# Fused tokenizer, attention and FFN: leaky ramps in one ScalarE instruction, queries placed by on-chip transfers, group loop unrolled, new order and banks

## The chip, the cores and the metric

The kernel runs on one core of a Trainium2 chip. A core has TensorE (PE), VectorE (DVE), ScalarE (ACT), GpSimd (POOL) and SyncE (SP, which here only issues transfers). The metric is the device time of one execution in microseconds, median of several runs.

## The reference, cut to what matters

64 images of 3 x 84 x 84 and 64 texts of 77 x 192 come in; the output has 64 x 102 x 192. For each image:

```python
h = leaky_relu(batchnorm(conv2d(x, stem_w, stem_b, 4)))      # 96 x 21 x 21, slope 0.01
offset = conv2d(h, off_w, off_b, 4)                          # 32 x 5 x 5
h = leaky_relu(batchnorm(deform_conv(h, offset, dcn_w, dcn_b)))   # bilinear samples: 25 tokens of 192
h = concatenate([h, txt])                                    # 102 tokens of 192
h = h + quantised_attention(layernorm(h))                    # 12 heads of 16, 8-bit q, k, v;
                                                             # softmax as integer exponential, probabilities powers of two
h = h + gelu(layernorm(h) @ in_w + in_b) @ out_w             # 768 hidden
```

`leaky_relu(x)` is x where x is at least 0 and 0.01 x elsewhere.

## The kernel before, in words

Images are worked on in 16 groups of four (`GRP`). Each engine runs a list of its own, written out by hand in the string `SLOT`: an entry such as `dve.STEM.3` reads engine, stage, lag, and means that in slot s the engine does this stage for image s - 3. All entries stand in one part of a slot of four, so one pass over the list serves one group; in a pass, stages of several groups are mixed. A lag counts only within its engine: there is no barrier between engines, which meet at semaphores alone. Stages in `PER_GROUP` are done once per group. The entries of one engine are executed strictly in their order, so an instruction that waits holds up all behind it. `walk` emits the passes: those up to slot 27 written out, then eight turns of a hardware loop (`Fori`, with counts computed from a register), then the rest written out.

The stages, in the order that a group goes through them:

- LX loads patches; STEM0 and STEM1 (PE, line 1089) are the first convolution of two images each. ACT's `stem` (line 571) writes 0.01 x the result to `LK`, DVE's `stem` (line 846) writes the maximum of the two to `H`.
- HTT transposes `H` in four pieces (L1095), OFF and OFS give the sampling offsets (L1111, L1118), POOL splits and masks them (OFS, RX; L511 to L532). HAT on PE (L1127, L1129), ACT (L601, L604) and DVE (L856) and HATW (L861) turn them into bilinear weights. INT (L1138, copied out at L613) samples. DCN (L1151) is the product with the second convolution's weights: ACT's `dcn` (L620) scales by 0.01 into `LKD`, DVE's `dcn` (L870) takes the maximum into `TOKB`, and SP stores it to a DRAM scratch (L472).
- LA loads tokens and texts into `XA`; LN1, RS1 and LN1X normalise (L883 to L902, L550), the product with the weights for v is V0 and V1 (L1171, L1174, rounded at L644), for q and k FQ0 and FQ1 (L1198, L1204, rounded at L652, L654).
- QKC on DVE (`qk_cast`, lines 919 to 937) casts q to `QB` and k to `KK`, then builds the block matrix `Q0`/`Q1`: twelve `tensor_scalar` multiply all rows of q by a column of `own` that is 1 in the rows of one head and 0 elsewhere. SC on PE multiplies by `KK` (L1215, L1218) and waits for it.
- The softmax goes between ACT (SC L664, SQ L671, LOG L678, PR L686), DVE (SC, MAX, BND, QQ, QQG, REM, EP, EXP, SUM, RCP, PW, PR; L943 to L1026) and POOL (MAX, L542).
- PV1, PV2, PV3 are the probabilities' transposition, product with v and output projection (L1230, L1239, L1249), RES the residual (L1045) on `XR`, loaded by LR; LN2, LN2X, FFN0 to FFN2 and FF2 the second half (L1182, L1186, L1264, L1052); YO0 and YO1 store the output.

PSUM has eight banks: two for the scores and six shared by all other products by the table `BANKS`; before PE writes to one, `BankUse.take` makes it wait until the bank's last result has been read. DVE also prepares weights in the head: `sampling_constants` after the fourth STEM, then behind the first four HATW in turn `fold_bn2`, `scalars`, `qkv_integers`, `qkv_weights`, and `proj_weights` behind the first DCN.

Of the kernel before, what the change touches and what calls it, by code (L numbers as in the profile page):

```python
# [65 lines left out]
dve.SUM.15 act.LN1X.10 pe.FF2.21 dve.RCP.15 act.HTT.5 dve.REM.14 pe.PV3.19 dve.EP.14 act.LN1X.9  # L66
pool.RX.4 pe.PV2.17 dve.HAT.8 act.PV2.12 dve.BND.13 pe.HAT.10 dve.HATW.8 act.LN1X.8 dve.QQ.13
sp.LA.12 pe.FF2.20 act.STEM.2 dve.EXP.14 dve.QQG.13 pe.PV3.18 act.V.11 dve.EP.13 pe.LN1X.15
act.HTT.4 dve.REM.13 dve.SUM.14 pool.RS2.12 act.V.10 pe.HTT.9 dve.V.13 dve.RCP.14 act.FQ0.8
pe.PV1.16 dve.PW.15 act.FQ1.8 dve.SC.12 pe.LN1X.14 dve.PR.15 act.HAT.5 dve.MAX.12 pe.PV3.17  # L70
act.SC.11 dve.EXP.13 pe.PV2.16 dve.SUM.13 act.LN2X.15 pool.MAX.11 dve.RCP.13 pe.LN1X.13 act.STEM.1
dve.PW.14 sp.LX.0 dve.FF2.19 act.SC.10 pe.HTT.8 dve.PR.14 act.V.9 dve.BND.12 pe.LN1X.12 dve.QQ.12
act.LN2X.14 pe.V0.12 dve.DCN.8 act.STEM.0 dve.QQG.12 pe.PV3.16 pool.MAX.10 dve.REM.12 act.INT.7
dve.PW.13 pe.FQ0.12 act.LN2X.13 dve.PV2.15 dve.PR.13 pe.FQ1.12 act.SC.9 dve.EP.12 pe.INT.11
act.HTT.3 dve.EXP.12 dve.FF2.18 act.LN2X.12 pe.HAT.9 dve.SUM.12 dve.RCP.12 act.INT.6 pool.MAX.9
pe.SC.15 sp.LR.12 dve.LN1.8 act.V.8 dve.FF2.17 pe.STEM1.4 dve.PV3.15 act.HAT.4 dve.RES.15 pe.LN2X.19
act.SQ.11 dve.STEM.3 pe.SC.14 dve.LN1X.11 act.FFN0.12 dve.PV2.14 pe.LN2X.18 act.FFN1.12 dve.LN1X.10
pool.MAX.8 dve.PW.12 act.SC.8 pe.V1.12 dve.FF2.16 act.FFN2.12 dve.PR.12 pe.SC.13 dve.PV3.14
act.SQ.10 pe.LN2X.17 dve.HAT.7 act.HTT.2 dve.RES.14 pe.HTT.7 dve.PV2.13 act.INT.5 dve.LN1X.9
sp.YO0.20 pe.INT.10 pool.OFS.0 act.LOG.11 dve.V.12 dve.LN1X.8 pe.LN2X.16 act.PR.11 dve.HATW.7  # L80
pe.SC.12 act.OFF.0 dve.PV3.13 dve.PV2.12 act.SQ.9 pe.HAT.8 dve.RES.13 dve.HAT.6 act.INT.4 pe.HTT.6
dve.PV3.12 act.LOG.10 dve.V.11 pool.RX.3 pe.FFN0.16 dve.RES.12 act.OFS.0 dve.LN2.12 pe.FFN1.16
act.PR.10 dve.STEM.2 pe.FFN2.16 dve.V.10 act.PV1.11 dve.LN2X.15 pe.INT.9 act.LOG.9 dve.QKC.8
sp.YO1.20 dve.HATW.6 act.DCN.4 pe.OFF.4 dve.HAT.5 pool.RX.2 act.PV2.11 dve.LN2X.14 pe.INT.8
dve.SC.11 act.PR.9 pe.FF2.19 dve.LN2X.13 act.PV1.10 dve.MAX.11 pe.PV1.15 dve.SC.10 act.SQ.8
dve.STEM.1 pe.OFS.4 act.PV2.10 dve.LN2X.12 dve.BND.11 pe.DCN.8 act.STEM.-1 pool.RX.1 dve.MAX.10
pe.PV2.15 act.PV1.9 dve.QQ.11 dve.STEM.0 act.HAT.3 pe.STEM0.0 dve.EP.11 dve.BND.10 act.LOG.8
pe.PV1.14 sp.DCN.8 dve.QQG.11 act.PR.8 dve.SC.9 pe.FF2.18 dve.REM.11 act.HAT.2 dve.QQ.10 pe.PV2.14
pool.RS1.4 act.PV2.9 dve.HATW.5 pe.PV1.13 dve.EXP.11 act.LN1X.7 dve.MAX.9 pe.HAT.7 act.PV1.8
# [15 lines left out]
W1_STEPS, SAMPLING_STEPS, BN2_STEPS, QKV_STEPS, PREP_STEPS = 7, 12, 17, 58, 74


class BankUse:
# [4 lines left out]

    def take(self, t, k, drained, per, plus=None):


# [1 line left out]
        value = per * t.n + (per if plus is None else plus + 1)
        step = per * (1 if t.per_group else GRP)
        if t.turn is not None and b not in self.entered:  # L120

            self.entered[b] = self.last[b]
        if b in self.last:
            before, at, by, looped = self.last[b]
            if t.turn is not None:
                self.pe.wait_ge(before, t.turn * by + at)
            else:
                if looped:
                    at += by * (TURNS - 1)
                self.pe.wait_ge(before, at)  # L130
        self.last[b] = (drained, value, step, t.turn is not None)

    def check(self):

        for b, (before, at, by, _) in self.entered.items():
            drained, value, step, _ = self.last[b]
            assert drained is before and value == at + by and step == by, b


class Turn:  # L140


    def __init__(self, n, i, per_group, banks, turn):
        self.n, self.i, self.per_group, self.banks, self.turn = n, i, per_group, banks, turn
# [1201 lines left out]
```

## Time and profile before

| | us |
|---|---|
| median of 3 runs (lowest, highest) | 1175.64 (1172.16, 1175.76) |
| the profiled execution's own time | 1170.16 |
| its span in the trace | 1168.4 |

The profile is one execution, seen by instruction. Busy time of an engine is the union of its instructions' times, without waiting. PEclk is the clock that TensorE was granted, 1.00 being 2.4 GHz and 0.50 being 1.2 GHz. "Idle before" names the instruction whose semaphore released the waiting engine last. SPq is SP's own queue of issues.

### The profile page before, as it was taken

How to read it: one execution, taken by the hardware profiler on the slowest of the kernel's cores; microseconds unless marked ns; L12 is line 12 of the kernel's file. 1: busy time of each engine (PE TensorE's matmuls, PEld its weight loads, DVE VectorE, ACT ScalarE, POOL GpSimd, SP SyncE). 2: the span in 40 equal slices, each digit the busy share in tenths (PEclk: the TensorE clock that was granted, in tenths of full speed). 3: DMA queues.
4: the chain of work that ended last, by engine and by line, in shares of the span. 5: the costliest groups of instructions: out<-in, count | busy, mean ns of one | idle time of the engine just before them, and what ended most of it. 6: DMA issues, size and time to landing. Idle time of an engine off the chain costs nothing. (4 is left out here: it accounts for less than half of the span.)

```text
span 1168.4 us, 21251 instructions
## 1 busy us (share of the span) xinstructions
PE 991.8 (85%) x6306; PEld 604.7 (52%) x6306; DVE 998.8 (85%) x2187; ACT 868.9 (74%) x1969; POOL 274.5 (23%) x241
## 2 busy tenths in 40 slices
...
GB/s 169 17 14 23 3 13 24 14 35 14 34 14 34 4 28 16 14 33 13 33 13 33 13 22 11 13 33 13 33 13 34 14 22 2 36 1 36 1 11 11
...
## 3 DMA queue, kind: packets, MB, share of 16 engines
...
q14 instruction: 30, 0.25, 0.1%
...
## 5 line engine op out<-in xcount | busy, mean ns | idle before, releaser
L542 POOL TENSOR_TENSOR m_sb<-mx_sb,a_sb 128x1020 f16<-128x1020 f16 x64 | 143.0, 2235 | 487.2 <-DVE mx_sb L955 487.2
L1138 PE MATMUL bank<-hats_sb,ht_sb 126*96 126x400 f32 (+1 forms) x512 | 212.9, 550 | 15.0 <-DVE hats_sb L861 12.7
L678 ACT ACTIVATE ee_sb<-ee_sb,rs_sb 128x102 f32<-128x102 f32 x640 | 180.1, 383 | 1.3 <-DVE rs_sb L1011 1.3
L1264 PE MATMUL bank<-w_out_sb,ge_sb 128*102 128x192 f32 x768 | 140.2, 333 | 7.2 <-DVE y_sb L1052 3.2
L1138 PEld LDWEIGHTS bank<-hats_sb,ht_sb 126*96 126x96 f32 (+1 forms) x512 | 78.5, 173 | 127.2 <-issue 107.4
L1264 PEld LDWEIGHTS bank<-w_out_sb,ge_sb 128*102 128x102 f32 x768 | 122.6, 170 | 20.9 <-issue 16.8
L861 DVE TENSOR_TENSOR hats_sb<-hats_sb 126x1600 f32<-126x1600 f32 x64 | 116.5, 1820 | 0.1
L604 ACT ACTIVATE hats_sb<-bank 126x400 f32<-126x400 f32 x256 | 107.9, 519 | 0.6 <-PE bank L1129 0.6
L998 DVE SCALAR_TENSOR_TENSOR ee_sb<-sq_sb,sc_sb,ep_sb 128x1020 f32<-128x1020 f32 x64 | 81.6, 1275 | 24.4 <-ACT sq_sb L671 24.2
L625 ACT ACTIVATE xt_sb<-bank 128x204 f32<-128x204 f32 x128 | 44.6, 349 | 63.7 <-PE bank L1161 62.4
L1151 PE MATMUL bank<-wdcn_sb,samp_sb 96*100 96x192 f32 (+1 forms) x512 | 88.4, 332 | 0.5 <-ACT samp_sb L613 0.5
L550 POOL TENSOR_TENSOR rstd_sb<-ve_sb,half_sb 102x4 f32<-102x4 f32 x32 | 33.4, 1043 | 231.3 <-DVE ve_sb L892 231.3
L1230 PE MATMUL bank<-ident_sb,p_sb 128*102 128x128 bf16 x640 | 58.8, 232 | 32.3 <-ACT o_sb L701 17.8
L664 ACT ACTIVATE a_sb<-scores,sc_sb 128x1020 f16<-128x1020 f32 x64 | 71.4, 1115 | 18.1 <-PE scores L1218 13.0
L1151 PEld LDWEIGHTS bank<-wdcn_sb,samp_sb 96*100 96x100 f32 (+1 forms) x512 | 84.2, 171 | 1.1 <-issue 0.6
L532 POOL TENSOR_TENSOR rx_sb<-offs_sb,mask_sb 96x400 bf16<-96x400 bf16 x64 | 60.3, 952 | 95.9 <-PE bank L1129 94.0
L694 ACT ACTIVATE pt_sb<-bank 102x640 bf16<-102x640 bf16 (+1 forms) x128 | 80.4, 686 | 1.3 <-PE bank L1230 1.3
L1182 PE MATMUL bank<-xt_sb,w_in_sb 128*128 128x408 f32 x192 | 80.5, 543 | 0.6 <-ACT xt_sb L625 0.5
L671 ACT ACTIVATE sq_sb<-rm_sb,sc_sb 128x1020 f32<-128x1020 f16 x64 | 73.8, 1152 | 8.0 <-DVE rm_sb L983 7.4
L1006 DVE TENSOR_REDUCE ss_sb<-ee_sb 128x10 f32<-128x1020 f32 x64 | 77.3, 1207 | 1.8
L856 DVE TENSOR_SCALAR hats_sb<-hats_sb 126x2000 f32<-126x2000 f32 x64 | 76.0, 1188 | 1.6 <-ACT hats_sb L604 1.5
L1161 PE MATMUL bank<-ident_sb,xh_sb 102*128 102x102 f32 x256 | 56.1, 307 | 20.8 <-DVE xh_sb L902 16.7
...
## 6 DMA issues: line engine op xcount, KB each, us to landing
xc_sb<-x_col SPq DMA_DIRECT2D x32, 165.4 KB, 2.9
...
```

The source lines that it names most:

```text
L542: nc.gpsimd.tensor_tensor(M16[b][:], MX[b][:].unsqueeze(2).to_broadcast([128, RT, TOK]), A16[b][:], ALU.subtract).then_inc(m_done, 1)
L604: nc.scalar.activation(HATS[b][:, 1 + j, :], bank[t.banks[1]][0:CH, 0:SMP], ACT.Abs, bias=float(-ROWS * j)).then_inc(ay_done, 1)
L678: last = nc.scalar.activation(EE[b][:, r, :], EE[b][:, r, :], ACT.Ln, scale=RS[b][:, r:r + 1])
L694: nc.scalar.activation(PT[:, k * (RT // 2 * 128):k * (RT // 2 * 128) + n], bank[t.banks[k]][0:TOK, 0:n // 2].bitcast(bf16), ACT.Copy).then ...
L856: v.tensor_scalar(HATS[b][:], HATS[b][:], -1.0, 0.0, ALU.add, ALU.min).then_inc(hat_done, 1)
L861: v.tensor_tensor(HATS[b][:, 1:, :], HATS[b][:, 1:, :], HATS[b][:, 0:1, :].to_broadcast([CH, NCH, SMP]), ALU.mult).then_inc(w_done, 1)
L998: v.scalar_tensor_tensor(EE[b][:].rearrange("p h k -> p (h k)"), SQ[:], sc[:, CC:CC + 1], EP[:].bitcast(bf16), ALU.add, ALU.mult).then_inc ...
L1006: v.tensor_reduce(SS[b][:], EE[b][:], AX.X, ALU.add).then_inc(ss_done, 1)
L1138: last = mm(bank[t.banks[0]][0:C1, 0:SMP], HT[0:rows, t.i, j, :], HATS[b][0:rows, 1 + j, :], start=(j == 0), stop=(j == NCH - 1))
L1151: last = mm(dst, SAMP[rows, k, :, :].rearrange("c g p -> c (g p)"), WD[rows, k, :], start=(k == 0), stop=(k == TAPS - 1))
L1182: mm(bank[t.banks[c]][:, 0:GRP * TOK], weights(k + c, c), src[:, c, :], start=True, stop=False)
L1264: last = mm(bank[t.banks[0]][0:TOK, 0:D], GE[:, f, t.i * TOK:(t.i + 1) * TOK], WOUT[:, f, :], start=(f == 0), stop=(f == FT - 1))
```

## The change

1. Both leaky ramps become one ACT instruction, `Prelu` with `alpha=SLOPE`, straight from PSUM to `H` and to `TOKB`. DVE's stages STEM and DCN and the tiles `LK`, `LKD` go. ACT's ramp now waits for the readers of `H` of the group before (OFF and HTT), and for the store of `TOKB`.
2. The twelve multiplications of QKC and `own` go. A new stage QD on SP copies each head's 16 rows of `QB` to its place in `Q0`/`Q1` by a transfer inside SBUF; the zeros around stay from POOL's fill. Scores wait for these twelve transfers besides `KK`.
3. `Fori` goes: `walk` writes all passes out, and `Turn`, `BankUse` and the counts lose their register forms.
4. `SLOT` and `BANKS` are new. DVE prepares `sampling_constants` and `scalars` before its list, then `fold_bn2`, `qkv_integers`, `qkv_weights`, `proj_weights` behind the first four HATW.

```diff
 def stem(t):                                    # ACT
-    b = t.i % 2
     act.wait_ge(h_full, t.count(1, 1))
-    if t.n >= 2:
-        act.wait_ge(h_done, t.count(1, -1))
-    nc.scalar.activation(LK[b][:], bank[...][0:C1, 0:NPIX], ACT.Copy, scale=SLOPE).then_inc(lk_done, 1)
+    if t.n < 1:
+        act.wait_ge(fill_s, FILL_H)
+    if t.n >= GRP:
+        act.wait_ge(off_full, t.of_group(1, 0))
+        act.wait_ge(ht_full, t.count(1, 1 - GRP))
+    nc.scalar.activation(H[:, t.i, 0:NPIX], bank[...][0:C1, 0:NPIX], ACT.Prelu, alpha=SLOPE).then_inc(h_done, 1)
 def dcn(t):                                     # ACT
     act.wait_ge(dcn_full, t.count(1, 1))
     if t.n >= 1:
-        act.wait_ge(tok_done, t.count(1, 0))
-    nc.scalar.activation(LKD[:], bank[t.banks[0]][0:GRP * POS, 0:D], ACT.Copy, scale=SLOPE).then_inc(lkd_done, 1)
+        act.wait_ge(tok_out, t.count(16, 0))
+    nc.scalar.activation(TOKB[:], bank[t.banks[0]][0:GRP * POS, 0:D], ACT.Prelu, alpha=SLOPE).then_inc(tok_done, 1)
-def stem(t):                                    # DVE
...
-    v.tensor_tensor(H[:, t.i, 0:NPIX], bank[...][0:C1, 0:NPIX], LK[b][:], ALU.max).then_inc(h_done, 1)
-def dcn(t):                                     # DVE
...
-    v.tensor_tensor(TOKB[:], bank[t.banks[0]][0:GRP * POS, 0:D], LKD[:], ALU.max).then_inc(tok_done, 1)
+sampling_constants()
+scalars()
 def weights(t):
...
-        (fold_bn2, scalars, qkv_integers, qkv_weights)[t.n]()
+        (fold_bn2, qkv_integers, qkv_weights, proj_weights)[t.n]()
 def qk_cast(t):
     dve.wait_ge(qk8_done, t.count(4, 4))
...
+    if t.n >= 1:
+        dve.wait_ge(q_in, t.count(16 * NH, 0))
     v.tensor_copy(QB[:], QK8[:, 0:2, :]).then_inc(qb_done, 1)
...
-    v.tensor_copy(KK[0:64, 1, :], QK8[64:128, 1, :])
-    dve.wait_ge(qb_done, t.count(1, 1))
-    for h in range(NH):
...
-        last = v.tensor_scalar(dst[:, :, at:at + TOK], QB[0:rows, block, :].rearrange("p (g q) -> p g q", q=TOK),
-                               own[0:rows, own_h:own_h + 1], None, ALU.mult)
-    last.then_inc(qk_done, 1)
+    v.tensor_copy(KK[0:64, 1, :], QK8[64:128, 1, :]).then_inc(qk_done, 1)
+def place_queries(t):                           # SP
+    sp.wait_ge(qb_done, t.count(1, 1))
+    if t.n < 1:
+        sp.wait_ge(fill_s, FILLS)
+    else:
+        sp.wait_ge(score_full, t.count(GRP, 0))
+    for h in range(NH):
+        dst, block, at = (Q0, 0, h * TOK) if h < FIRST_HEADS else (Q1, 1, h * TOK - 128 * CROSS)
+        rows = slice(h % FIRST_HEADS * HD, h % FIRST_HEADS * HD + HD)
+        sp.dma_start(dst[rows, :, at:at + TOK],
+                     QB[rows, block, :].rearrange("p (g q) -> p g q", q=TOK)).then_inc(q_in, 16)
 def scores(t):                                  # PE
     pe.wait_ge(qk_done, t.of_group(1, 1))
+    pe.wait_ge(q_in, t.of_group(16 * NH, 16 * NH))
-BANKS = dict(STEM0=(2, 0), STEM1=(4, 5), HTT=(2,), OFF=(3,), OFS=(0,), HAT=(4, 3), INT=(1,),
-             DCN=(4,), LN1X=(5,), LN2X=(3,), V0=(3, 1), V1=(2, 0), FQ0=(5, 1), FQ1=(4, 5),
-             PV1=(3, 1), PV2=(1,), PV3=(4,), FFN0=(0, 4), FFN1=(1, 3), FFN2=(5, 0), FF2=(5,))
+BANKS = dict(STEM0=(3, 4), STEM1=(5, 0), HTT=(2,), OFF=(5,), OFS=(0,), HAT=(0, 3), INT=(1,),
+             DCN=(0,), LN1X=(4,), LN2X=(4,), V0=(0, 3), V1=(2, 3), FQ0=(4, 2), FQ1=(5, 1),
+             PV1=(3, 5), PV2=(1,), PV3=(5,), FFN0=(4, 5), FFN1=(0, 3), FFN2=(2, 1), FF2=(2,))
```

The new list, PE's and SP's entries of one pass in their order:

```
pe: INT.11 STEM1.4 V1.12 LN2X.19 SC.15 HTT.8 LN2X.18 SC.14 LN2X.17 INT.10 LN2X.16 HTT.7 HAT.8 SC.13 HTT.6 FFN0.16 SC.12
    FFN1.16 FFN2.16 OFF.4 INT.9 STEM0.0 FF2.19 INT.8 PV1.15 DCN.8 PV2.15 PV1.14 OFS.4 FF2.18 PV2.14 FF2.17 PV1.13 HAT.7
    PV3.15 FF2.16 LN1X.11 HAT.6 PV2.13 HTT.5 PV3.14 LN1X.10 PV1.12 LN1X.9 V0.8 LN1X.8 PV2.12 PV3.13 FQ0.8 FQ1.8 HAT.5 PV3.12
sp: LR.12 LX.0 YO0.20 DCN.8 LA.8 YO1.20 QD.8
```

## Rows read from the trace of the kernel before

**Rows 1.** Page, part 1: busy us, share of the span, instructions.

```profile
PE 991.8 (85%) x6306; PEld 604.7 (52%) x6306; DVE 998.8 (85%) x2187; ACT 868.9 (74%) x1969; POOL 274.5 (23%) x241
```

**Rows 2.** Windows: stretch, length; busy PE, PEld, DVE, ACT, POOL; PEclk; DMA; GB/s.

```profile
274.80:338.40 63.60, 57.19 (x392) 35.22 (x393) 59.85 (x133) 54.06 (x125) 16.33 (x14) 1.00 0.08 23
...
536.20:603.30 67.10, 61.98 (x396) 37.94 (x397) 60.04 (x133) 53.96 (x124) 16.46 (x14) 0.92 0.07 20
603.30:667.00 63.70, 57.72 (x396) 35.35 (x396) 59.89 (x133) 54.08 (x124) 16.36 (x14) 1.00 0.08 21
...
209.20:992.40 783.20, 715.76 (x4729) 440.19 (x4727) 723.15 (x1586) 647.56 (x1478) 200.49 (x169) 0.96 0.07 21
```

**Rows 3.** Windows of one microsecond, same columns.

```profile
562.00:563.00 1.00, 0.00 (x0) 0.00 (x0) 1.00 (x5) 1.00 (x4) 0.00 (x0) 1.00 0.00 0
...
565.00:566.00 1.00, 1.00 (x10) 0.71 (x11) 1.00 (x2) 0.67 (x3) 0.00 (x0) 0.50 0.00 0
```

**Rows 4.** PE's timeline in one group: start, us, instruction; idle before it.

```profile
624.81 0.62 PE L1204 MATMUL bank<-xt_sb,wqk_sb 64*128 64x204 f32 x4
625.36 3.10 PE L1138 MATMUL bank<-hats_sb,ht_sb 126*96 126x400 f32 x8
...
630.29 0.49 PE L1215 MATMUL scores<-kk_sb,q_sb 128*128 128x102 bf16 x7 [1.35 <-DVE q_sb L935]
```

**Rows 5.** Waits in total: engine, line, releaser: us, times, longest.

```profile
DVE tokb_sb L870 <- ACT lkd_sb L620: 31.8, 16, 6.9
```

**Rows 6.** Groups by line and shape: count | busy us, mean ns | idle before, releaser.

```profile
L846 DVE TENSOR_TENSOR h_sb<-bank,lk_sb 96x441 f32<-96x441 f32 x64 | 38.7, 608 | 17.5 <-ACT lk_sb L571 17.3
...
L1171 PE MATMUL bank<-wv_sb,xt_sb 128*102 128x192 f32 x128 | 34.3, 402 | 0.0
...
L571 ACT ACTIVATE lk_sb<-bank 96x441 f32<-96x441 f32 x64 | 33.9, 536 | 26.2 <-PE bank L1089 26.2
...
L935 DVE TENSOR_SCALAR q_sb<-qb_sb,own_sb 128x408 bf16<-128x408 bf16 x128 | 31.6, 321 | 0.2
...
L935 DVE TENSOR_SCALAR q_sb<-qb_sb,own_sb 64x408 bf16<-64x408 bf16 x64 | 16.3, 311 | 0.0
```

**Rows 7.** The tile `tokb`: count, duration min/median/max, first and last start.

```profile
L870 DVE TENSOR_TENSOR tokb_sb<-bank,lkd_sb x16: 357/358/358, 77.0 to 1056.7; 100x192 f32<-100x192 f32 x16
...
L472 SPq MOVE tok_scratch<-tokb_sb x8: 29/29/29, 405.6 to 861.9; - x8
```

**Rows 8.** SP's queue, timeline of the first 150 us.

```profile
5.99 1.35 SPq L394 DMA_DIRECT2D offb_sb<-off_b  x3
...
77.39 0.32 SPq L472 DMA_DIRECT2D tok_scratch<-tokb_sb  x1
79.08 0.27 SPq L453 DMA_DIRECT2D xa_sb<-tok_scratch  x1
```

**Rows 9.** DVE's timeline at the place of rows 4.

```profile
626.06 0.58 DVE L926 CAST qb_sb<-qk_sb 128x816 bf16<-128x816 int8 x1 [0.26 <-ACT qk_sb L654]
```

**Rows 10.** Head, PE's timeline.

```profile
21.41 0.65 PE L1118 MATMUL bank<-offq_sb,fold_sb 128*96 128x100 f32 x2 [0.37 <-ACT offq_sb L585]
32.24 1.79 PE L1089 MATMUL bank<-xc_sb,stem_w_sb 49*96 49x441 f32 x4 [10.18 <-DMA xc_sb<-x_col]
```

**Rows 11.** Head, POOL's timeline.

```profile
24.39 1.67 POOL L532 TENSOR_TENSOR rx_sb<-offs_sb,mask_sb 96x400 bf16<-96x400 bf16 x2
```

**Rows 12.** Head, DVE's timeline.

```profile
46.89 1.81 DVE L861 TENSOR_TENSOR hats_sb<-hats_sb 126x1600 f32<-126x1600 f32 x1
...
54.47 1.20 DVE L856 TENSOR_SCALAR hats_sb<-hats_sb 126x2000 f32<-126x2000 f32 x1
...
86.01 0.88 DVE L883 BATCH_NORM_STATS2 st_sb<-xa_sb 102x6 f32<-102x192 f32 x3
```

**Rows 13.** Page, part 6: issues, KB each, median us to landing.

```profile
xc_sb<-x_col SPq DMA_DIRECT2D x32, 165.4 KB, 2.9
```

**Rows 14.** Chain that ended last, in order of time: start, us, what.

```profile
1079.56 2.67 DVE q_sb L935 x11
```

More of the change, by code:

```diff
@@ L65 @@
 |
[L66 to L89, printed above, removed]
@@ L90 @@
-dve.QQG.10
+dve.HAT.0 act.FQ1.8 pe.INT.11 dve.QQ.5 act.V.10 dve.HATW.0 pe.STEM1.4 dve.QQG.5 act.INT.7 pool.RX.5
+pe.V1.12 dve.EXP.6 act.HAT.5 dve.REM.5 pe.LN2X.19 sp.LR.12 dve.SUM.6 act.V.9 dve.RCP.6 pe.SC.15
+act.LN2X.15 dve.PW.7 pe.HTT.8 act.SC.11 dve.EP.5 dve.SC.4 pe.LN2X.18 act.HTT.4 dve.PR.7 pool.RS1.8
+act.LN2X.14 dve.MAX.4 pe.SC.14 dve.EXP.5 act.LN2X.13 pe.LN2X.17 dve.SUM.5 act.SC.10 dve.RCP.5
+pe.INT.10 dve.FF2.11 act.STEM.1 dve.BND.4 pe.LN2X.16 act.STEM.0 dve.PW.6 sp.LX.0 pe.HTT.7 dve.QQ.4
@@ new lines @@
+act.V.8 pool.RS2.12 dve.PR.6 pe.HAT.8 act.INT.6 dve.QQG.4 act.LN2X.12 dve.V.5 pe.SC.13 dve.REM.4
+act.HTT.3 pe.HTT.6 dve.EP.4 act.HAT.4 dve.EXP.4 pe.FFN0.16 dve.SUM.4 act.SC.9 dve.V.4 pe.SC.12
+pool.RX.4 act.HTT.2 dve.PV2.7 pe.FFN1.16 dve.RCP.4 act.SQ.11 dve.PW.5 pe.FFN2.16 sp.YO0.20
+act.FFN0.12 dve.FF2.10 dve.PR.5 pe.OFF.4 act.SC.8 dve.FF2.9 act.FFN1.12 pe.INT.9 dve.LN1.0
+dve.LN1X.3 act.FFN2.12 pool.MAX.11 pe.STEM0.0 dve.PW.4 act.OFF.0 dve.LN1X.2 pe.FF2.19 act.SQ.10
+dve.PV2.6 pe.INT.8 dve.PV3.7 act.LOG.11 dve.PR.4 pe.PV1.15 act.INT.5 dve.RES.7 dve.FF2.8 pe.DCN.8
@@ new lines @@
+act.STEM.-1 dve.HAT.-1 pool.MAX.10 sp.DCN.8 act.PR.11 pe.PV2.15 dve.PV3.6 dve.LN1X.1 act.SQ.9
+pe.PV1.14 dve.RES.6 act.LOG.10 dve.LN1X.0 pe.OFS.4 dve.PV2.5 act.INT.4 pe.FF2.18 dve.HATW.-1
+act.PV1.11 dve.PV3.5 pe.PV2.14 pool.MAX.9 act.PR.10 dve.HAT.-2 dve.PV2.4 pe.FF2.17 act.LOG.9
+dve.HATW.-2 pe.PV1.13 act.SQ.8 dve.V.3 dve.QKC.0 act.DCN.4 sp.LA.8 pe.HAT.7 dve.RES.5 act.PR.9
+dve.PV3.4 pe.PV3.15 dve.V.2 act.STEM.-2 pool.MAX.8 pe.FF2.16 dve.RES.4 act.PV2.11 dve.LN2.4
+pe.LN1X.11 dve.LN2X.7 act.PV1.10 dve.HAT.-3 pe.HAT.6 act.OFS.0 dve.HATW.-3 pe.PV2.13 dve.LN2X.6
@@ new lines @@
+act.LOG.8 dve.LN2X.5 act.PV2.10 pe.HTT.5 dve.SC.3 pool.OFS.0 act.PV1.9 dve.MAX.3 pe.PV3.14 sp.YO1.20
+dve.LN2X.4 act.PR.8 pe.LN1X.10 dve.SC.2 act.HAT.3 dve.BND.3 pe.PV1.12 dve.QQ.3 act.LN1X.7 dve.MAX.2
+pe.LN1X.9 act.HAT.2 dve.QQG.3 pe.V0.8 dve.REM.3 act.PV2.9 pool.RX.3 dve.EP.3 pe.LN1X.8 act.LN1X.6
+dve.BND.2 dve.SC.1 act.PV1.8 pe.PV2.12 dve.QQ.2 act.LN1X.5 pe.PV3.13 dve.EXP.3 act.LN1X.4 dve.MAX.1
+sp.QD.8 pe.FQ0.8 dve.EP.2 act.HTT.1 dve.SUM.3 pe.FQ1.8 pool.RX.2 act.PV2.8 dve.RCP.3 pe.HAT.5
+dve.QQG.2 act.V.7 dve.BND.1 pe.PV3.12 act.FQ0.4 dve.REM.2
```

114 lines of the change are left out of this document (32 added, 82 removed).

## The prediction, made before the changed kernel was run

> **What bounds the kernel now.** I read the engine totals first [rows 1]: PE 991.8 and DVE 998.8 us busy in a span of 1168.4, both 85%, ACT 74%. An average over stages can't say who binds, so I cut the span by group of four images (one token store of SP to the next) and asked for busy time in each stretch [rows 2]. From 209.2 to 992.4 there are 12 full groups, 783.2 us, 65.27 us a group. In them PE is busy 715.76 / 12 = 59.6, DVE 723.15 / 12 = 60.3 and ACT 647.56 / 12 = 54.0 us. Single groups come in two kinds. Where the granted clock is 1.00 throughout (603.3 to 667.0, 63.7 us), DVE is idle 3.8 us and PE 6.0: DVE binds. Where the clock averages 0.92 (536.2 to 603.3, 67.1 us), PE is busy 61.98 and idle 5.1, DVE idle 7.1: PE binds. The finer windows show that the clock falls from 1.00 to 0.50 (2.4 to 1.2 GHz) some 3 us after a microsecond in which PE ran nothing [rows 3]; that empty microsecond is the wait of the first score matmul for the queries that DVE places [rows 4]. In that list of events PE's wait was 1.35 us. By the waits in total [rows 5] DVE also stood 31.8 us behind ACT's `lkd`, 2.0 a group.
>
> **The change, part by part.**
>
> *Leaky ramps.* Each was an ACT scaling and a DVE maximum. DVE loses 64 maxima of 608 ns, 38.7 us [rows 6], and 16 of 358 ns, 5.7 us [rows 7]. ACT keeps as many instructions: 64 of 536 ns [rows 6] become 64 Prelu of the same shape. No Prelu is in the trace. Bounds from the nearest rows: 0 if it costs what the scaling costs, and 64 x (608 - 536) = 4.6 us more if it costs what the maximum costs; below 0 nothing speaks, since the input and output are the same. I take 0, the row of the same engine. ACT at 54 of 65 us could hide 0.3 us a group either way. DVE's wait for `lkd`, 2.0 a group, goes: the store now waits for ACT directly.
> The Trainium skill, page "ScalarE: Activation LUTs", section "Step-by-step: what each stage is for", states that throughput is the same per element whatever the function; by it the price is 0 as well, no run here yet shows it for Prelu. The same page's "Rules for kernel authors" would leave maximum and multiply on VectorE, not ScalarE. By this case's rows the float32 ramp is not quicker there (608 against 536 ns), so the rule isn't borne out for this shape, and the measurement decides.
>
> *Queries.* DVE loses 192 multiplications, 31.6 + 16.3 = 47.9 us [rows 6]. All together DVE loses 38.7 + 5.7 + 47.9 = 92.3 us, 5.8 a group: 60.3 becomes 54.5. In their place SP issues 12 transfers of 16 partitions x 4 x 204 bytes inside the chip's SBUF. Three issues in a row took 1.35 us, 0.45 each, and the token store was followed by the load that waits for it 79.08 - 77.39 = 1.7 us later [rows 8]. The cast to `qb` starts at 626.06, 0.63 us after the last projection matmul ended (624.81 + 0.62), and takes 0.58 [rows 4, 9]. So queries lie in place 0.63 + 0.58 + 11 x 0.45 + 1.7 = 7.9 us after the last FQ1 matmul; before, the first score started 630.29 - 625.43 = 4.9 us after it. The bounds of this unseen chain: 1.2 + 11 x 0.32 + 1.7 = 6.4 below (every issue as short as the token store's), 1.2 + 12 x 1.7 = 21.6 above (no overlap between transfers). I take 7.9: three issues 0.45 apart are the nearest row.
> What covers it: the new order puts between FQ1 and the first score (SC.15) on PE: HAT.5, PV3.12, INT.11, STEM1.4, V1.12 and LN2X.19. INT is 3.1 us [rows 4] and the first half of V1 34.3 / 32 = 1.1 [rows 6]; four short groups and V1's other half come on top. So PE waits between 0 and 7.9 - 4.2 = 3.7; I take 1.5, close to the 1.35 of now. SP's queue behind the 12 issues holds the residual load and the next patches; both are due tens of microseconds later, and the cast's next turn waits for the landing only a group later.
> The Trainium skill, page "DMA: Bandwidth & Descriptors", section "Anatomy of one DMA", gives each transfer a fixed cost of about 2.0 us, and its rules say that this overlaps if the issue is early. The row's 1.7 us agrees for a single one; by 2.0 the chain would be 8.2 instead of 7.9. Its "Why small descriptors are slow" says that transfers inside SBUF are spared the penalty of small pieces; no row shows one.
>
> *Unrolling.* SP's register moves, one a turn, show 8 turns from 405.6 to 861.9 [rows 7]. An unrolled group of the kernel before (274.8 to 338.4) took 63.6 us, a looped one (603.3 to 667.0) 63.7 us, both at clock 1.00 [rows 2]. 8 x 0.1 = 0.8 us at most, I take 0.
>
> *New order and banks in the steady part.* PE does what it did. It becomes the bound: 59.6 busy a group with as many clock drops as now, 57.7 without any. To this comes its idle time. DVE, where it was alone the bound, idled 3.8; with that PE gives 63.4 with the drops and 61.5 without. Since the empty microsecond ahead of the scores stays about as long, but the other small waits of PE for DVE shrink, I take 62.5. Saved: 12 x (65.27 - 62.5) = 33.2 us. Three more group periods lie in the filling and draining of the pipe, where PE isn't the bound throughout: half of it each, 3 x 1.4 = 4.2.
>
> *Head.* OFS.4 now stands behind STEM0.0 on PE. Before, it ran at 21.41; STEM0 of the second group waited for its patches until 32.24 and ended at 34.0 [rows 10]. From its start to the end of POOL's first masked copy lay 24.39 + 0.84 - 21.41 = 3.8 us [rows 10, 11], so the first hats on PE, which followed STEM0 at 34.0, now come near 37.8, 3.8 later. Against it, the 30 tiny scalar steps that DVE did between the hats of images 1 and 2 (48.7 to 54.47, 5.8 us [rows 12]) now run before, while DVE waits; the integer steps move up in their place, and the projection weights, which stood behind the first tokens, go ahead of them. The first store comes out within 1 us of 77.4. LN1 of the first group, though, started only at 86.01, behind those projection weights (77.36 to 86.0) [rows 12]; now it starts with its tokens, 79.4 + 2.9 (a load's landing [rows 13]) = 82.3, less the 0.5 of the shorter ramp: 4.2 us gained. The first queries arrive 7.9 - 4.9 = 3.0 later: together -1.2.
>
> *Tail.* After the last store (1056.7 [rows 7]) everything hangs on one chain: the queries took 2.67 us of it on DVE [rows 14] after the casts of the keys. Transfers make that 3.0 longer, nothing hides it; the shorter ramp gives 0.6 back: +2.4.
>
> *Sum.* 1168.4 - 33.2 - 4.2 - 1.2 + 2.4 = 1132.2 of span. The profiled execution took 1170.16, 1.8 over its span: 1134. The median of the runs was 1175.64, 5.5 above that execution; part of it may stay, so I say 1135.
>
> **Rivals.**
> *A, the clock stays up.* If the work that now lies ahead of the scores closes the gap, the drops go: 57.7 busy + 3.2 idle = 60.9. 12 x 4.4 + 3 x 2.2 = 59.4: 1168.4 - 59.4 + 1.2 + 1.8 = 1112. For it: groups at 1.00 exist now, and they have the same gap of 1.35 us, so it is on the edge. Against it: a denser PE leaves less slack for anything late.
> *B, slower: the placement becomes the bound.* Every microsecond by which the queries land later than 7.9 stops PE, since scores stand in its fixed order. The gain of 2.8 a group is gone at 10.7 us, that is at 0.68 us per transfer instead of 0.45. At 0.85 us each it is 12.3: 4.4 more idle, and with so long a gap every group gets a full drop (61.98 instead of 59.6 busy, 2.4): 62.5 + 6.8 = 69.3, and 15 x 4.0 = 60 us over now: 1230. For it: twelve transfers of 64 short pieces in one queue, never measured here. Against it: the issues came 0.45 apart, and the store landed within 1.7.
> *C, the work goes but the time stays.* PE, DVE and ACT are all near 54 to 60 of 65, each in a fixed order and with single banks; PE's 5.6 idle a group may be made of waits that only change their names (STEM1 and V1 now take banks from the hats, which ACT reads behind INT). Then a group stays 65.2 and only the edges move: 1168.4 + 1.2 + 1.8 = 1171. The ramps could also be no ramps of one instruction if Prelu needed its own table; its loads would show, and would land here too.
>
> **How the numbers follow.** My forecast (62 to 63.5 a group, 1120 to 1147) has 0.50, A (down to 1098) 0.25, C (1147 to 1175) 0.14, B 0.11. The measurement can't tell less than about 0.3%, 3.5 us, from no change. Faster: 0.50 + 0.25 + 0.08 of C = 0.83; same 0.05; slower 0.12. The range goes from 1098, A's end, to 1168, into C, and leaves out B and part of C.
>
> **What would show it.** Right: DVE near 907 us busy, ACT near 869, PE near 985 in a span of about 1132; group periods near 62.5 in the steady part; Prelu at 536 ns; PE waiting for transfers some 1.5 us a group; no DVE wait in front of the store; LN1 of the first group near 82; still clock drops in some groups. Wrong: PE idle above 5 us a group, a landing more than 9 us after FQ1, more ACT table loads than before, or DVE or ACT still the one that others wait for.

## The result, and the profile after

The changed kernel takes 1230.13 us (median of 4 runs, 1224.06 to 1235.03) against 1173.9 for the kernel before (median of 4), a ratio of 1.0484, 95% interval 1.0445 to 1.0523: 4.8% slower, where 1135 us was forecast. The profiled execution took 1235.03, its span is 1233.2.

The engine totals (page, part 1) answer [rows 1]:

```profile
PE 1022.4 (83%) x6306; PEld 629.8 (51%) x6306; DVE 911.1 (74%) x1914; ACT 863.9 (70%) x1969; POOL 263.6 (21%) x241
```

DVE lost 87.7 us, nearly the 92.3 forecast. The span grew by 65, and PE, which does the same work, is busy 31 us longer. Twelve groups between token stores, and three single microseconds in one of them, answer [rows 2, 3] (columns as there):

```profile
217.91:1052.31 834.40, 744.82 (x4728) 462.03 (x4727) 656.46 (x1379) 643.28 (x1476) 190.28 (x168) 0.92 0.08 22
```
```profile
666.00:667.00 1.00, 0.00 (x0) 0.00 (x0) 1.00 (x1) 0.34 (x1) 0.00 (x0) 1.00 0.12 21
...
669.00:670.00 1.00, 0.37 (x5) 0.20 (x4) 0.22 (x1) 1.00 (x2) 0.00 (x0) 0.81 1.07 347
670.00:671.00 1.00, 1.00 (x11) 0.72 (x9) 0.93 (x3) 0.36 (x2) 0.00 (x0) 0.50 0.62 160
```

A group takes 834.40 / 12 = 69.5 us instead of 65.27. PE is busy 62.1 of it at a mean clock of 0.92 and idle 7.5; DVE is idle 14.8. An empty microsecond of PE (666) is followed by the drop to 1.2 GHz some 3 us later, as before. Windows of 1 us over the 12 groups show the clock below 1.00 in 22 separate stretches here, and in 8 in the kernel before. Where the empty microsecond comes from is in the timeline of that place (start, us, instruction; idle before it), which answers [rows 4, 9]:

```profile
657.02 0.62 PE L1158 MATMUL bank<-xt_sb,wqk_sb 64*128 64x204 f32 x4
...
658.27 0.58 DVE L887 CAST qb_sb<-qk_sb 128x816 bf16<-128x816 int8 x1 [0.83 <-ACT qk_sb L637]
...
658.88 7.62 SPq L446 DMA_DIRECT2D q_sb<-qb_sb  x12
...
667.84 0.47 PE L1170 MATMUL scores<-kk_sb,q_sb 128*128 128x102 bf16 x7 [1.88 <-issue]
```
```profile
q_sb<-qb_sb SPq DMA_DIRECT2D x192, 12.8 KB, 1.9
```

Twelve issues take 7.62 us, 0.635 each, and a transfer lands after 1.9 (page, part 6). The first score starts 667.84 - 657.64 = 10.2 us after the last FQ1 matmul, where [rows 4] gave 4.9. "issue" here is the wait for these transfers.

The ramp into `H` (groups by line, as [rows 6]; 533 ns against 536 taken) and the first group's LN1 (head, as [rows 12]) came out as forecast; the ramp into `TOKB` is the second line:

```profile
L554 ACT ACTIVATE h_sb<-bank 96x441 f32<-96x441 f32 x64 | 32.1, 533 | 27.2 <-PE bank L1043 27.2
...
L603 ACT ACTIVATE tokb_sb<-bank 100x192 f32<-100x192 f32 x16 | 5.4, 337 | 20.2 <-PE bank L1105 20.2
```
```profile
82.70 0.88 DVE L846 BATCH_NORM_STATS2 st_sb<-xa_sb 102x6 f32<-102x192 f32 x3 [7.30 <-DMA xa_sb<-txt]
```

All that was lost lies between the first tokens and the last ones (tile `tokb`, as [rows 7]):

```profile
L603 ACT ACTIVATE tokb_sb<-bank x16: 312/332/353, 76.4 to 1120.8; 100x192 f32<-100x192 f32 x16
```

From 76.4 to 1120.8 are 15 group periods, 1044.4 us; before it was 1056.7 - 77.0 = 979.7. That is 64.7 more, where 33.2 + 4.2 + 1.2 = 38.6 less was forecast. The start is 0.6 us shorter, and the tail (1233.2 - 1120.8 = 112.4, before 111.7) 0.7 longer.

The waits of the steady part (214 to 1107 us; us in total, times, longest) hold one that the kernel before didn't have, of DVE for the output store:

```profile
DVE y_sb L1006 <- DMA out<-y_sb: 39.2, 12, 4.0
...
PE scores L1170 <- issue: 24.7, 13, 3.1
...
PE bank L1105 <- ACT samp_sb L596: 16.6, 12, 1.4
PE bank L1049 <- DVE y_sb L1006: 14.8, 13, 1.2
```

SP's queue and DVE in one group show how (timeline):

```profile
637.02 0.30 SPq L452 DMA_DIRECT2D tok_scratch<-tokb_sb  x1
...
638.71 0.26 SPq L420 DMA_DIRECT2D xa_sb<-tok_scratch  x1
639.01 0.34 SPq L421 DMA_DIRECT2D xa_sb<-txt  x1
639.40 0.36 SPq L458 DMA_DIRECT2D out<-y_sb  x1
...
643.81 0.36 DVE L1006 TENSOR_TENSOR y_sb<-bank,x_sb 102x192 f32<-102x192 f32 x1 [3.00 <-DMA out<-y_sb]
```

In the new list YO1 stands behind DCN and LA. The second output store is held back until the tokens have gone out and landed, and DVE can't write the next `Y` for 3.0 us.

### The profile page after: what moved, and what is told of

Read it like the earlier page. It is cut to its first block and busy times, and to the rows that moved or that the text cites. A ratio compares the mean times of both kernels' runs of the same rounds, so it can differ in the third digit from the quotient of the medians.

```text
span 1233.2 us, 20058 instructions
## 1 busy us (share of the span) xinstructions
PE 1022.4 (83%) x6306; PEld 629.8 (51%) x6306; DVE 911.1 (74%) x1914; ACT 863.9 (70%) x1969; POOL 263.6 (21%) x241
## 5 line engine op out<-in xcount | busy, mean ns | idle before, releaser
L1092 PE MATMUL bank<-hats_sb,ht_sb 126*96 126x400 f32 (+1 forms) x512 | 228.9, 585 | 10.3 <-ACT samp_sb L596 5.1
L1092 PEld LDWEIGHTS bank<-hats_sb,ht_sb 126*96 126x96 f32 (+1 forms) x512 | 86.6, 188 | 122.9 <-issue 117.2
L1105 PE MATMUL bank<-wdcn_sb,samp_sb 96*100 96x192 f32 (+1 forms) x512 | 103.9, 370 | 20.6 <-ACT samp_sb L596 20.6
L1105 PEld LDWEIGHTS bank<-wdcn_sb,samp_sb 96*100 96x100 f32 (+1 forms) x512 | 95.6, 192 | 26.7 <-ACT samp_sb L596 22.0
L596 ACT ACTIVATE samp_sb<-bank 96x400 f32<-96x400 f32 x64 | 32.5, 508 | 106.0 <-PE bank L1092 106.0
L897 DVE TENSOR_SCALAR a_sb<-a_sb 128x1020 f16<-128x1020 f16 x64 | 31.7, 495 | 72.8 <-ACT a_sb L647 72.7
```

The source lines that it names most:

```text
L1092: last = mm(bank[t.banks[0]][0:C1, 0:SMP], HT[0:rows, t.i, j, :], HATS[b][0:rows, 1 + j, :], start=(j == 0), stop=(j == NCH - 1))
L1105: last = mm(dst, SAMP[rows, k, :, :].rearrange("c g p -> c (g p)"), WD[rows, k, :], start=(k == 0), stop=(k == TAPS - 1))
```

## The experiments

Each time stands beside runs of the kernel before on the same chip. "Late" is the time from the end of the last FQ1 matmul to the first score (median of 12 groups), "idle" PE's mean idle time just ahead of that score, "group" the mean of 12 periods between token stores, "falls" the number of separate stretches with a clock below 1.00 in windows of 1 us over the 12 groups. All but the first three columns come from one traced execution each; for a_dveq it was 12.6 us faster than the median, for a_split 6.3 faster, for a_q1_yo1 5.5 slower, for the others within 5. Differences of up to some 4 us between two medians say little.

| kernel | us | ratio (95%) | late | idle | group | PE busy a group | clock | falls |
|---|---|---|---|---|---|---|---|---|
| b_unroll | 1174.93 | 1.0010 (0.9987, 1.0032) | 4.9 | 1.4 | 65.3 | 59.3 | 0.96 | 8 |
| b_prelu_unroll | 1169.16 | 0.9962 (0.9939, 0.9985) | 4.9 | 1.4 | 65.2 | 59.2 | 0.96 | 8 |
| b_m1 | 1143.05 | 0.9756 (0.9704, 0.9808) | 3.3 | 0.0 | 63.8 | 58.3 | 0.98 | 7 |
| b_qd_unroll | 1275.47 | 1.0850 (1.0809, 1.0892) | 10.2 | 6.7 | 71.7 | 60.6 | 0.92 | 12 |
| b_prelu_qd_unroll | 1269.13 | 1.0798 (1.0757, 1.0840) | 10.2 | 6.7 | 71.7 | 60.6 | 0.92 | 12 |
| after | 1230.13 | 1.0484 (1.0445, 1.0523) | 10.2 | 1.9 | 69.5 | 62.1 | 0.92 | 22 |
| a_dveq | 1226.8 | 1.0469 (1.0430, 1.0508) | 10.2 | 0.0 | 68.5 | 59.7 | 0.93 | 13 |
| a_yo1 | 1218.76 | 1.0398 (1.0345, 1.0451) | 10.2 | 1.8 | 68.2 | 61.6 | 0.93 | 18 |
| a_dveq_yo1 | 1222.41 | 1.0402 (1.0360, 1.0443) | 10.2 | 0.0 | 69.2 | 60.8 | 0.92 | 19 |
| a_early | 1192.03 | 1.0150 (1.0112, 1.0188) | 9.3 | 1.1 | 66.9 | 60.7 | 0.95 | 16 |
| a_q6_yo1 | 1168.41 | 0.9933 (0.9896, 0.9970) | 8.2 | 0.0 | 65.2 | 59.7 | 0.96 | 13 |
| a_q1_yo1 | 1166.53 | 0.9927 (0.9886, 0.9968) | 8.4 | 0.0 | 65.8 | 60.6 | 0.95 | 15 |
| a_split | 1173.28 | 0.9987 (0.9961, 1.0013) | 8.2 | 0.0 | 65.2 | 59.5 | 0.97 | 10 |
| b_best | 1145.7 | 0.9762 (0.9736, 0.9789) | 4.4 | 0.9 | 63.6 | 57.6 | 0.99 | 2 |
| b_best_mix | 1145.15 | 0.9764 (0.9730, 0.9799) | 3.6 | 0.2 | 63.7 | 58.2 | 0.98 | 6 |

### First: parts undone and parts done alone

**b_unroll**, the kernel before with its loop written out.

```diff
-    for slot in range(FIRST_SLOT, LOOP_FROM):
...
+    for slot in range(FIRST_SLOT, LAST_SLOT + 1):
         run_slot(name, slot, stages)
```

> The kernel before with the loop over groups written out and nothing else. All theories: no change within 0.3% (an unrolled group took 63.6 us and a looped one 63.7 in the trace): 1170 to 1178. If the longer program cost fetches, some 10 us more would show, and would be part of the loss.

1174.93 against 1174.46 for the kernel before: unrolling is worth nothing.

**b_prelu_unroll**, that and the Prelu ramps, in the order and on the banks of before; `proj_weights` stands behind the fourth HATW.

```diff
-    nc.scalar.activation(LK[b][:], bank[...][0:C1, 0:NPIX], ACT.Copy, scale=SLOPE)
+    nc.scalar.activation(H[:, t.i, 0:NPIX], bank[...][0:C1, 0:NPIX], ACT.Prelu, alpha=SLOPE)
-dve.STEM.0 ... dve.STEM.3 ... dve.DCN.8
```

> The kernel before, unrolled, with the two ramps as one Prelu each (DVE's maxima out of its list, all else in its order and banks; the ramps now wait on ACT for the readers of H; the projection weights are prepared behind the fourth hats). By the step of the prediction that DVE binds in groups at full clock and loses 2.8 us of work and 2.0 of waiting a group: 1135 to 1155. By the rival that PE, DVE and ACT hold each other in a fixed order and the work removed only becomes idle time: 1165 to 1176.

1169.16, 5.8 us below b_unroll, and the group as long as ever. In the traces the gain (1170.6 to 1167.0) lies ahead of the first tokens, written at 75.5 instead of 79.3; the 15 periods behind them take 979.4 against 979.5. Its 12 groups (windows), and who waits instead (waits in total):

```profile
208.69:990.49 781.80, 710.48 (x4724) 439.32 (x4724) 712.74 (x1525) 647.66 (x1477) 202.36 (x169) 0.96 0.08 22
```
```profile
DVE ee_sb L974 <- ACT sq_sb L664: 25.2, 22, 3.6
...
PE scores L1191 <- DVE q_sb L911: 22.5, 14, 4.9
...
DVE p_sb L995 <- ACT rr_sb L679: 18.4, 31, 1.6
```

DVE has four maxima of 0.6 us fewer in each group, and stands waiting for ACT longer: the first of these waits was 20.0 us in b_unroll. PE's wait for the queries stayed. Followed back from 990 us instruction by instruction to what released each, the chain reaches 476 us; of these 514 us, 211 lie on ACT, 172 on PE, 72 on DVE, and 57 have no releaser in the trace. By this walk DVE, at 84% busy, was not the bound; b_m1 below corrects how little it leaves to DVE.

**a_dveq**, the changed kernel with the twelve multiplications back on DVE instead of the transfers.

```diff
-sp.QD.8
+    for h in range(NH):
...
+        last = v.tensor_scalar(dst[:, :, at:at + TOK], QB[0:rows, block, :]..., own[0:rows, own_h:own_h + 1], None, ALU.mult)
```

> The changed kernel, with the twelve multiplications of DVE back in place of the twelve transfers of SP; order, banks, ramps and unrolling stay as changed. Theory 1 (the placement): 12 issues of 0.63 us and a landing of 1.9 make the first score of each group wait some 2 us and keep a clock drop in each group; with DVE's 2.9 us in their place 2 to 4 us a group come back: 1170 to 1200. Theory 2 (the output store that stands behind the token store in SP's queue, 42 us of DVE's waits): that wait stays, and DVE gets 2.9 us a group more: 1225 to 1240. Theory 3 (the new order and banks as such): 1215 to 1230.

1226.8, hardly less than the changed kernel. Read alone, this clears the transfers, and it misled me. PE no longer waits just ahead of the scores, but in the new list these multiplications stand ahead of other work that PE waits for (below).

**a_yo1**, the changed kernel with YO1 right behind YO0 in SP's list.

```diff
-sp.YO0.20 ... sp.YO1.20
+sp.YO0.20 sp.YO1.20
```

> The changed kernel, with one entry of SP's list moved: the second output store (YO1) stands right behind the first (YO0), ahead of the token store and of the load that waits for it. Theory 1 (placement): nothing changes, 1225 to 1235. Theory 2 (the store): DVE's 42 us of waiting for the output store and what PE waits behind it go, 2 to 3 us a group: 1185 to 1205. Theory 3 (order and banks): 1220 to 1232.

1218.76, which none of the three theories gave: the store's place is worth 11 us. DVE's 39 us of waiting for `out` are gone, 26.6 us of waiting for PE's product at the same line stand there instead.

### Second: order or placement

**a_dveq_yo1**: both edits together.

> The changed kernel with both suspects taken back: the twelve multiplications on VectorE instead of the twelve transfers, and the second output store right behind the first. What is left of the change is Prelu, the unrolled loop, and the new order with its banks. Order theory: these last two are what costs, so about 1209 us (1226.8 less the 11 that moving the store gave), between 1202 and 1218. Rival, that the two suspects cover for each other (each alone gave little because the other then came last): they go together for far more than 7.5 + 11 us, to 1185 or below.

1222.41, neither. Multiplications put back cost as much as transfers, and PE now waits elsewhere (waits in total; in a_yo1 this wait is 0.3):

```profile
PE bank L1126 <- DVE xh_sb L867: 36.5, 27, 1.9
```

Twelve multiplications hold DVE for 2.9 us, and the normalized tokens `xh` that PE transposes stand behind them. Transfer or multiplication, what costs in this order is what comes late behind it.

**a_q1_yo1**: a_yo1 with one of the twelve heads placed.

```diff
-    for h in range(NH):                         # place_queries
+    for h in range(1):
```

> The changed kernel with the second output store moved up, and only one of the twelve heads' queries placed in a group: eleven transfers are left out, so eleven of twelve heads are scored against zero queries. Placement then costs one issue of 0.6 us instead of 7.6. Order theory: PE's wait ahead of the scores goes (23 us of it in the run that moved the store) but the rest of the order holds, 1195 to 1207 us. Placement theory (rival B of the prediction): the transfers are what made it slow, and the time falls to 1180 or below, level with the kernel before.

1166.53, 52 us less. Leaving out eleven transfers takes all of a_yo1's loss away, and my theory that the order alone had caused it fell. Eleven heads have zero queries here, as in b_m1, and six in a_q6_yo1; a_split and b_best, which have the queries of all twelve and nearly the same times (1173.28, and 1145.7 beside b_m1's 1143.05), speak against the zeros as what makes these kernels fast.

**b_qd_unroll** and **b_prelu_qd_unroll**: the kernel before, unrolled, without and with Prelu, with the transfers in place of the multiplications, in the old order.

```diff
+sp.QD.12 sp.LX.0
+    pe.wait_ge(q_in, t.of_group(16 * NH, 16 * NH))
```

> The kernel before, loop written out, with the twelve multiplications on VectorE replaced by twelve transfers from SP's queue at the same place of the order (order and banks untouched, ramps untouched). Order theory: placement costs at most a few us, 1172 to 1182. Placement theory: each group's scores come 2 to 3 us later and PE waits for it 15 times, 1205 or more. The prediction's own sum (VectorE's 48 us go and come off the time) would give about 1150.

> Every part of the change but the new order and banks: Prelu ramps, twelve transfers, loop written out, in the order and on the banks of the kernel before. Order theory: near the run with Prelu alone, 1165 to 1178 us, so that the difference to the changed kernel (55 us) is the order's. Placement theory: 1200 or more. The prediction's central step (time follows VectorE's busy time, which falls here by over 90 us as it does in the changed kernel): 1135 or below.

1275.47 and 1269.13: 100 us up in the old order, which has little between FQ1 and the scores. A group grows by 6.4 us, where the placement theory reckoned with 2 to 3 (windows, and the waits in total, of b_qd_unroll):

```profile
224.37:1084.58 860.21, 726.73 (x4724) 450.27 (x4724) 695.98 (x1441) 646.92 (x1478) 199.47 (x168) 0.92 0.08 22
```
```profile
PE scores L1213 <- issue: 80.8, 12, 7.0
```

80.8 / 12 = 6.7 us a group, where b_unroll's idle is 1.4: 5.3 of the 6.4 by which the group grew. The new order has 8.2 us of PE's work in that place instead of 3.3 ("late" where nothing is waited for), so it hides some 5 us more of the transfers' lateness, yet not all.

### Third: lateness or load

**a_early**: a_yo1 in which the cast of the queries waits for the two rounded blocks it reads instead of for all four.

```diff
-    dve.wait_ge(qk8_done, t.count(4, 4))
+    dve.wait_ge(qk8_done, t.count(4, 2))
     v.tensor_copy(QB[:], QK8[:, 0:2, :]).then_inc(qb_done, 1)
+    dve.wait_ge(qk8_done, t.count(4, 4))
```

> The changed kernel with the second output store moved up, and the cast of the queries released by the first two of ScalarE's four rounded blocks (the two it reads) instead of by all four. In the trace of the run that only moved the store the cast starts at 646.89, while its two blocks were ready at 645.76: 1.1 us earlier in each group. Theory now: the scores come when the last of the twelve transfers has landed, and this, not VectorE's work, is what the changed kernel waits for. Then it gives 15 times 1.1, about 1202 us (1196 to 1210). Rival, that the transfers cost by something other than their lateness (they load the memories or SP's queue): no difference, 1215 to 1222.

1192.03. Less than one microsecond a group earlier ("late" 10.2 to 9.3) gave 27 us in all, more than the 16 of the lateness theory. The traces' 12 groups differ by 16.0 us, of which 11.0 are PE's busy time (739.03 to 728.02): less idle here came with less time at 1.2 GHz. The other 11 us of the medians lie outside these 12 groups or in the spread of the runs.

**a_split**: a_early with the last five transfers issued from ACT's queue.

```diff
+act.V.10 act.QDA.8
-    for h in range(NH):                         # SP
+    for h in range(7):
+    for h in range(7, NH):                      # ACT, place_rest
+        act.dma_start(...).then_inc(q_in, 16)
```

> As the run before in this list, with the last five of the twelve transfers issued from ScalarE's queue, where it stands 3.6 us idle ahead of L596 in the trace, and seven from SP's. The last query then lands 5 times 0.6 = 3.0 us earlier, in all 4.1 us, more than the 1.9 to 3.3 us for which PE's path waits. Lateness theory: nearly all that leaving out eleven transfers gave comes back, 1170 to 1180 us. Load theory: as many bytes and transfers as ever, so 1195 or above; and if ScalarE's issues cost its path (15 times 3 us), above 1215.

1173.28. As many bytes and transfers as ever, and 45 of the 52 us between a_yo1 and a_q1_yo1 are gained: 27 by the early cast, 19 by the second queue. The timeline of one group (ACTq is ACT's own queue of issues):

```profile
552.95 0.62 PE L1171 MATMUL bank<-xt_sb,wqk_sb 64*128 64x204 f32 x4
553.28 0.58 DVE L899 CAST qb_sb<-qk_sb 128x816 bf16<-128x816 int8 x1
...
553.89 4.44 SPq L446 DMA_DIRECT2D q_sb<-qb_sb  x7
553.89 0.61 ACTq L649 DMA_DIRECT2D q_sb<-qb_sb  x1
554.53 2.84 ACTq L649 DMA_DIRECT2D q_sb<-qb_sb  x4
557.96 0.52 ACT L596 ACTIVATE samp_sb<-bank 96x400 f32<-96x400 f32 x1 [3.58 <-PE bank L1105]
...
561.72 0.48 PE L1183 MATMUL scores<-kk_sb,q_sb 128*128 128x102 bf16 x7
```

The last issue ends at 558.33, and with 1.9 to landing, counted from its start at 557.7, the queries are there at 559.6; PE comes at 561.72 without having waited. Four of ACT's five issues lie in its idle 3.58 us.

**a_q6_yo1**: as a_q1_yo1, six heads placed.

> The changed kernel with the store moved up and six of the twelve heads placed (six left out, scored against zero queries): the last lands 3.6 us earlier than with twelve. With one transfer it was 1166.5, with twelve 1218.8. Lateness theory: the first few transfers are free and each of the others costs 0.6 us a group, so about 1170 (1164 to 1178). Load theory: in proportion to the number, 1190 (1186 to 1196).

1168.41, as with one: the first six are free, the other six cost 50. Not a load, a deadline. Windows of a_yo1 and of a_q6_yo1:

```profile
216.86:1035.11 818.25, 739.03 (x4730) 458.61 (x4729) 658.40 (x1380) 641.62 (x1476) 189.89 (x168) 0.93 0.09 23
```
```profile
211.88:994.38 782.50, 716.71 (x4734) 450.42 (x4732) 660.71 (x1380) 642.76 (x1476) 188.46 (x168) 0.96 0.08 23
```

Of the 35.75 us between them, 739.03 - 716.71 = 22.3 are PE running the same matmuls longer at the lower clock, the other 13.4 idle.

**b_m1**: b_prelu_unroll with one of the twelve multiplications (the other heads' queries stay zero).

```diff
-    for h in range(NH):
+    for h in range(1):
```

> The kernel before with Prelu ramps and the loop written out, and one of the twelve multiplications left (eleven heads' queries are left out and stay zero): VectorE loses 44 us more, and nothing takes its place. It tells whether the multiplications were on the path of the kernel before, by the place at which they stand (between the projections and the scores) and not by VectorE's load. If they were, the time falls by about 3 us a group, to 1115 to 1130 us, which is what a free placement would have been worth. If the chain goes round them through ScalarE and PE, as the walk through the trace says (VectorE holds 14% of it), 1155 to 1168.

1143.05, between the two: 26 us below b_prelu_unroll for 44 us of multiplications. The walk back had given DVE too little: it follows one chain and doesn't see the clock. The clock accounts for 10.4 of the 16.3 us that the 12 groups gained (PE busy 710.48 to 700.05).

### Fourth: the kernel before, with its queries earlier

**b_best**: b_prelu_unroll with the early cast, the multiplications right behind it, and the key casts, the first of which needs the later blocks, last. The earlier wait and the new sequence were not run apart.

```diff
-    dve.wait_ge(qk8_done, t.count(4, 4))
+    dve.wait_ge(qk8_done, t.count(4, 2))
     v.tensor_copy(QB[:], QK8[:, 0:2, :]).then_inc(qb_done, 1)
-    v.tensor_copy(KK[:, 0, :], QK8[:, 2, :])
-    v.tensor_copy(KK[0:64, 1, :], QK8[64:128, 1, :])
     for h in range(NH):
...
+    dve.wait_ge(qk8_done, t.count(4, 4))
+    v.tensor_copy(KK[:, 0, :], QK8[:, 2, :])
+    v.tensor_copy(KK[0:64, 1, :], QK8[64:128, 1, :]).then_inc(qk_done, 1)
```

> The kernel before with Prelu ramps and the loop written out (1169.16 us), in which the queries' cast is released by the two rounded blocks it reads, and the twelve multiplications stand ahead of the two casts of the keys, which wait for the last two blocks. VectorE's instructions are the same in kind and number. Lateness theory: the queries and keys are ready about 1.1 us earlier in each group, 15 times, so 1150 to 1157 us. Load theory: no difference, 1166 to 1172.

1145.7, ratio 0.9762 (0.9736 to 0.9789): faster than both kernels and below the 1150 to 1157 expected, with every multiplication kept, and nearly as good as leaving eleven of them out. Its 12 groups (windows), and the place in one of them (timeline):

```profile
202.73:965.80 763.07, 691.60 (x4724) 427.39 (x4724) 709.00 (x1525) 646.46 (x1477) 205.09 (x168) 0.99 0.08 22
```
```profile
606.85 0.61 PE L1180 MATMUL bank<-xt_sb,wqk_sb 64*128 64x204 f32 x4
...
607.54 0.58 DVE L902 CAST qb_sb<-qk_sb 128x816 bf16<-128x816 int8 x1
608.23 2.91 DVE L909 TENSOR_SCALAR q_sb<-qb_sb,own_sb 128x408 bf16<-128x408 bf16 x12
611.06 0.36 DVE L912 CAST kk_sb<-qk_sb 128x408 bf16<-128x408 int8 x1
611.43 0.37 DVE L913 CAST kk_sb<-qk_sb 64x408 bf16<-64x408 int8 x1
...
611.86 0.49 PE L1191 MATMUL scores<-kk_sb,q_sb 128*128 128x102 bf16 x7 [0.88 <-DVE kk_sb L913]
```

PE's idle stretch is 0.88 us here. The same place in b_prelu_unroll, and single microseconds of it (windows):

```profile
624.35 0.61 PE L1191 MATMUL scores<-kk_sb,q_sb 128*128 128x102 bf16 x7 [1.35 <-DVE q_sb L911]
```
```profile
623.00:624.00 1.00, 0.00 (x1) 0.00 (x0) 1.00 (x6) 1.00 (x3) 0.00 (x0) 1.00 0.00 0
...
626.00:627.00 1.00, 1.00 (x5) 0.12 (x2) 1.00 (x2) 0.56 (x1) 0.00 (x0) 0.50 0.00 0
```

Here the clock falls to 0.50 behind the 1.35 us idle; behind the 0.88 it is 1.00 in each of the seven microseconds from 610 to 617. This holds in most groups, not in all. In b_prelu_unroll PE is idle 1.35 us ahead of the scores in all 12 groups, and the clock falls behind it in 8; in b_best it falls in 2, once behind 1.23 us and once behind 0.88 with a second wait of 0.40. Over 12 groups the gain is 781.80 - 763.07 = 18.7 us, and PE's busy time falls by 710.48 - 691.60 = 18.9, while its idle time stays at 6.0 a group: in the steady part the whole gain is TensorE's clock.

**b_best_mix**: eight heads multiplied, two transferred from SP's and two from ACT's queue.

```diff
+sp.QD.12 sp.LX.0
+act.FQ1.8 act.QDA.8
-    for h in range(NH):                         # DVE
+    for h in range(8):
```

> The run before in this list with eight of the twelve heads multiplied on VectorE and two each transferred from SP's and ScalarE's queue at the same time: VectorE loses another 16 us, and the last transfer lands after two issues of 0.6 and 1.9 us, 3.1 us, against 2.0 + 0.75 us of multiplications and casts. Lateness theory: the transfers are now last by a little, but earlier than twelve multiplications by 0.6 us, so 1145 to 1157 us, up to 9 less than the run before. Load theory: 16 us off VectorE gives at most a few us, 1160 to 1170. If ScalarE's issues cost its path, above both.

1145.15, the same. The queries come 0.8 us earlier again and 16 us go off DVE, for nothing. Over the 12 groups PE is idle 5.5 us less and busy 6.5 us longer (691.60 to 698.11): the clock falls six times instead of twice, each time within 3 us of two waits of 0.5 to 0.6 us for ACT or transfers. Why it falls there more often stays open.

## Why the prediction was wrong

**What failed first: "DVE binds", and with it the steady group of 62.5.** I read 60.3 us of 65.27 [rows 2] as a bound and subtracted work. Taking the ramps off DVE shortened a group by 0.1 us. The multiplications were worth 1.4 a group (b_prelu_unroll to b_m1), and not as load: b_best gets 1.6 with all of them kept. What they cost was the 1.35 us ahead of the scores [rows 4] and the clock behind it, which I had named as the cause of the clock drop [rows 3] and then left at "about as long". In place of the forecast 62.5 the changed kernel has a group of 69.5, and no run came below 63.6.

**The wait for the placed queries, taken at 1.5, was 1.9 in `after`, and still mis-priced.** Both signs that the prediction named for this failure came: PE idle above 5 us a group (7.5) and a landing more than 9 us after FQ1. Placement came at 10.2 us after FQ1 instead of 7.9: an issue takes 0.635, not the 0.45 of three loads [rows 8], which is 11 x 0.185 = 2.0 of the 2.3 us. The Trainium skill, page "DMA: Bandwidth & Descriptors", section "Anatomy of one DMA", which the prediction cites, gives its 2.0 us for transfers that GpSimd issues. SP's transfers landed here after 1.9, close to it. The cover was larger than the 4.2 I could sum: where PE doesn't wait, it reaches the scores 8.2 after FQ1. The two errors nearly cancelled in the wait, by luck. What I missed is what an idle stretch of this length costs: between a_q6_yo1 and a_yo1 it is 1.8 us ahead of the scores, but 3.0 in the group.

**The new order and banks were taken at nothing.** Where neither kernel waits for queries (b_m1 and a_q6_yo1) the new order's group is 65.2 against 63.8, and the kernels differ by 25 us. PE is idle 5.5 us a group in both, and busy 59.7 against 58.3, so the whole difference is the clock, which falls 13 times against 7. The trace shows where (waits in total of a_q6_yo1):

```profile
PE bank L1105 <- ACT samp_sb L596: 19.4, 13, 1.6
```

L1105 is DCN's product, which waits for ACT's copy of the last samples, not for a bank. b_m1 has no such wait: the old list has FF2.19, PV1.15 and OFS.4 between INT.8 and DCN.8, the new one PV1.15 alone. Ten of the 13 falls begin within 3 us of the start of this wait. No run moved DCN or tried the order and the banks apart, so that this wait is what costs is read from the trace and not shown. It is close to rival C: waits that change their names, here at 1.4 us a group, and through the clock.

**An issue moved past others was not counted.** YO1 behind the token store costs 11 us (1.3 a group).

So the way from b_unroll (1174.9) to the changed kernel (1230.1) goes in these steps, each the difference of two runs (some from different chips, so good to about 4 us): Prelu -6, the multiplications out -26, new order, banks and six transfers +25, the other six transfers +50, YO1's place +11.

**The rivals.** B (1230) has the result's size and its mechanism, lateness that stops PE and drops the clock, but not its numbers: an issue was 0.635, below its threshold of 0.68 (by its own sum of eleven steps it is 2.8 / 11 above 0.45, so 0.70), and the landing at 10.2 short of its 10.7. Its group of 69.3 with PE busy 61.98 meets the measured 69.5 and 62.1 by luck: it puts 5.9 us of wait ahead of the scores, and 1.9 were there. It holds since the gain it had to eat up was never there. A named the right lever: b_best's PE is busy 57.6 us a group, its 57.7, and the group is 63.6 instead of its 60.9, since idle time stayed at 6.0; A's 3.2 of idle came from no row. Unrolling (0), Prelu's price (533 ns), DVE's busy time and the head (LN1 at 82.70) were right.
